# A spline evaluated from tables on TensorE: the far table is summed, and its part made, ahead of the near one

## The reference, cut to what matters

```python
out = relu(batchnorm(conv3x3(x, sign(w1)), gamma1, beta1))
out = batchnorm(conv3x3(out, sign(w2)), gamma2, beta2)
x = relu(out + x)                                  # the first layer's result

x_aff = clip(x * a[c] + b[c], -1.5, 1.5)           # the second layer, K = 32, R = 8
u = (x_aff + 1.0) * 0.5 * (K - 1)
i = floor(u); t = clip(u - i, 0, 1)
spline = sum over m of alpha_table[clip(i - 1 + m, 0, K - 1)] * b_m(t)      # four cubic basis functions
y = id_gain[c] * x + einsum('bchwr,cr->bchw', spline, mix) + bias[c]
```

## Time and profile before

| | |
|---|---|
| median of 3 runs | 1161.8 us (1159.59 to 1162.68) |
| time of the profiled execution | 1162.34 us |
| span of the profiled execution | 1160.5 us |
| TensorE matmuls busy | 1093.0 us |
| VectorE busy | 954.2 us |
| ScalarE busy | 909.4 us |
| chain that ended last | TensorE L1161 52%, L1170 8% |

### The profile page before, as it was taken

How to read it: one execution, slowest core, us unless ns; L and a number is a source line. 1 busy time by engine, 2 the same in 40 slices (tenths; PEclk the granted TensorE clock), 3 DMA queues, 4 the chain that set the end, 5 groups by cost and what they waited for, 6 DMA issues and landing times.

```text
span 1160.5 us, 51486 instructions
## 1 busy us (share of the span) xinstructions
PE 1093.0 (94%) x23818; PEld 751.4 (65%) x23818; DVE 954.2 (82%) x891; ACT 909.4 (78%) x451; POOL 138.6 (12%) x219
## 2 busy tenths in 40 slices
PE   6999999699999946999999999999999999999996
PEld 4678888578888833665666656665656766665664
DVE  5855656585665777999999999999999999999987
ACT  4435443678788627999999999999999999999971
POOL 7000000058000000011010110110110101101100
PEclk9999999899999977999999999999999999999998
DMA  6766765667767766899999989989999999999652
GB/s 229 260 257 256 278 241 224 229 236 279 278 256 281 289 249 169 189 218 228 220 218 230 218 214 236 220 216 237 215 220 222 213 230 212 225 217 219 147 134 85
DMA packets 58225, 260.95 MB, mean 225 GB/s; under 512 B 16336, under 2 KB 16336, under 8 KB 50000
## 3 DMA queue, kind: packets, MB, share of 16 engines
q1 hardware_dynamic: 48880, 209.20, 55.7%
q0 software_dynamic: 8640, 48.17, 22.7%
q10 hardware_dynamic: 544, 1.10, 0.3%
HBM read 104.29 MB, written 77.07 MB: 156 GB/s over the span
## 4 chain that ended last, share of the span: by engine, by line
PE 60%; DVE 1%; issue 1%; ACTq 0%; ACT 0%; DVEq 0%
PE tab L1161 52%; PE tab L1170 8%; ACTq L949 0%; DVE lin L1120 0%; DVE poly L1116 0%; DVE zbuf L1024 0%; DVE lin L1012 0%; DVE far_sq L1085 0%; DVE poly L1091 0%; DVE middle_mask L1046 0%; ACT zbuf L933 0%; ACT cell L941 0%; DVE lin L1018 0%; DVE offset L1032 0%; DVEq L1084 0%
## 5 line engine op out<-in xcount | busy, mean ns | idle before, releaser
L1161 PE MATMUL tab<-edge_mask,diag 128*32 128x392 bf16 x10240 | 446.8, 329 | 5.9 <-issue 5.9
L1161 PEld LDWEIGHTS tab<-edge_mask,diag 128*32 128x32 f16 x10240 | 277.1, 97 | 168.9 <-issue 28.4
L981 ACT ACTIVATE edge_mask<-cell,thr 128x6272 bf16<-128x6272 bf16 x62 | 338.6, 5508 | 0.5 <-DMA cell<-cell 0.5
L414 ACT ACTIVATE yout<-acc 128x1568 f32<-128x1568 f32 x64 | 94.2, 1472 | 163.0 <-PE acc L715 140.8
L1161 PE MATMUL tab<-middle_mask,diag 128*32 128x392 bf16 x4096 | 186.9, 332 | 26.8 <-DVE middle_mask L1046 22.9
L715 PE MATMUL acc<-band_split,w 64*64 64x392 f16 x4608 | 198.6, 330 | 9.9 <-ACT band_split L372 6.5
L715 PE MATMUL acc<-split,w 64*64 64x392 f16 x4608 | 196.5, 330 | 11.2 <-DVE w L467 9.7
L715 PEld LDWEIGHTS acc<-band_split,w 64*64 64x64 f16 x4608 | 164.3, 107 | 44.0 <-issue 14.8
L715 PEld LDWEIGHTS acc<-split,w 64*64 64x64 f16 x4608 | 154.5, 107 | 52.4 <-issue 11.8
L1161 PEld LDWEIGHTS tab<-middle_mask,diag 128*32 128x32 f16 x4096 | 110.3, 98 | 91.5 <-DVE middle_mask L1046 23.0
L524 DVE BATCH_NORM_STATS2 stats<-yout 128x392 f32 (+1 forms) x240 | 118.0, 555 | 60.8 <-ACT yout L414 60.0
(11 more groups left out here) (133 smaller groups left out, 956.2 us busy)
## 6 DMA issues: line engine op xcount, KB each, us to landing
y_scratch<-yout SPq DMA_DIRECT2D x32, 1568.0 KB, 6.2
cell<-cell SPq DMA_DIRECT2D x504, 98.0 KB, 5.0
xin<-y_scratch SPq DMA_DIRECT2D x16, 1568.0 KB, 9.1
lin<-far POOLq DMA_DIRECT2D x32, 784.0 KB, 9.5
out<-lin SPq DMA_DIRECT2D x31, 784.0 KB, 5.6
xin<-in_x SPq DMA_DIRECT2D x15, 1568.0 KB, 9.3
lin<-y_scratch SPq DMA_DIRECT2D x30, 784.0 KB, 9.5
lin<-in_x POOLq DMA_DIRECT2D x28, 784.0 KB, 7.7
```

Source lines behind the costliest of these rows:

```text
L414: act.activation(yout[b][:, :].rearrange("p (r k x) -> p k r x", r=2, k=TILES)[:, 2 * part:2 * part + 2], acc[:, 4 * part:4 * part + 4, 0: ...
L981: act.activation(mask_of(c, q)[:, :, :], cell4[c % 2][:, :, :], ACT.Sign, bias=thr[:, q:q + 1]).then_inc(sign_mask_ready, 1)
L1161: mm = pe.matmul(tab[(c + t) % 2][j * GROUP:(j + 1) * GROUP, sub, 0:SUB], keep["diag"][part][:, j % 2, t, q, :], mask_of(c, q)[:, j, sub * ...
```

## The change

The far table becomes the first table of a chunk and the near table the second. VectorE does `far_cube(c)` in the place where `near_cube(c)` stood, `far_part(c)` right behind `finish(c-1)`, and `near_cube(c)` behind `far_part(c)`. The first middle mask now waits for the near table, because that is the second one. By the new numbers `used(c, T_NEAR)` is 5c + 2 where it was 5c + 1, so the wait ahead of L1170 asks for the second table to have been used. The constants' small arrays are indexed by the same names, and the instructions that fill them stay as many.

```diff
-T_NEAR, T_FAR, T_SQ, T_LIN, T_VAL = range(TABLES)
+T_FAR, T_NEAR, T_SQ, T_LIN, T_VAL = range(TABLES)
...
             def middle(c, q):
 
                 dve.wait_ge(copied[c % 2], 256 * (c // 2 + 1))
-                dve.wait_ge(table_ready, used(c - 1, T_FAR))
+                dve.wait_ge(table_ready, used(c - 1, T_NEAR))
...
-                near_cube(c)
+                far_cube(c)
                 if c > 0:
                     finish(c - 1)
-                far_cube(c)
                 far_part(c)
+                near_cube(c)
                 if c + 1 < CHUNKS:
                     middle(c + 1, MIDDLE_QUADS[0])
                 square(c)
```

## The result

The changed kernel takes 1166.13 us (median of 20 executions, 1161.70 to 1168.02) against 1161.79 us for the kernel before on the same chips (20 executions, 1156.57 to 1169.46). The ratio is 1.0039, with a 95% interval of 1.0026 to 1.0051: slower by 0.4%, 4.3 us, where 9.5 us were forecast. The profiled execution took 1167.21 us, 4.87 us more than the one before.

The account below looks back on a forecast made before the run. TensorE's string of matmuls, 21.52 us a chunk, was taken as the bound; the change makes 29 x 22.12 + 6.12 = 647.60 us where there were 638.15, 9.45 more, so 1171.3 us, range 1164.5 to 1179.5.

Parts of the forecast that it names:

- The loop: Product at L1170, square, on to the next near_cube, product: 22.12 us a chunk, 0.60 us over TensorE's 21.52.
- chunks 30 and 31 don't pay: Without fixed and linear for a later chunk VectorE regains 2.0 us there; only chunks 1 to 29 pay.
- The handover: Near step to product's load 0.06 us, first load to next square 3.01 us; an exposed load adds at most 0.20.
- Nothing waits for far_sq, masks or the second table: At VectorE's steps and TensorE's mask loads, inputs come in time; the 0.54 us wait for the second table goes.
- The stops: TensorE's "issue" pieces, 14.07 us over 29 periods before; staying put, they exceed the new periods by 6.12 us.
- the sentence on `add_far`: GpSimd's far transfer is issued 2.5 us earlier in the chunk, while finish asks for it a whole chunk later.
- The second, in which the stops vanish behind the wait: Rival: TensorE's sequencer gets ahead while waiting, periods of 22.12 sharp, 3.3 us more, 1165.1 us; chance 0.10.
- Stops in full: Rival: no wait covers TensorE's stops, each of 29 periods gets 0.60 us, 17.4 us more, 1179.2 us; chance 0.13.
- faster: Rival: stops covered and a shorter loop through near_cube, 21.88 us a chunk, 3.6 us less, 1158.2 us; chance 0.04.
- it doesn't bite: Rival: TensorE reaches the product late enough in every chunk for other reasons, time unchanged at 1161.8 us; chance 0.06.

Follow-up runs that it names:

- e1: The changed kernel with near_cube put back ahead of far_part, the far table still first: 1161.77 us, ratio 0.9993 to the kernel before.
- e7: The changed kernel with GpSimd holding add_far until near_cube is done: 1170.31 us, ratio 1.0078 to the kernel before.
- e12: Repeat of e7 beside e11, the changed kernel with add_far held until near_cube is done: 1171.46 us, ratio 1.0075 to the kernel before.
- e11: The changed kernel once more, nothing altered, beside e12: 1165.73 us, ratio 1.0034 to the kernel before.
- e3: The changed kernel with add_far held until the next chunk's first middle mask is made: 1168.53 us, ratio 1.0059 to the kernel before.
- e2: The changed kernel with finish moved last, behind near_cube, and far_part_added split into one semaphore per buffer: 1150.75 us, ratio 0.9899 to the kernel before.
- e8: e2 with add_far held until near_cube is done: 1156.92 us, ratio 0.9961 to the kernel before.
- e6: e2 with add_far held until finish is done: 1161.09 us, ratio 1.0002 to the kernel before.
- e5: e1 with add_far held until the next chunk's first middle mask is made: 1170.15 us, ratio 1.0076 to the kernel before.
- e4: The kernel before with copies of the cells cut to 32 of 1568 pixels from chunk 2 on, for timing alone: 1149.72 us, ratio 0.9891.
- e10: The kernel before with its far transfer cut to 32 of 1568 pixels in every chunk, for timing alone: 1148.93 us, ratio 0.9893.

## Why the prediction was right in its mechanism and wrong in its size

**The loop: right.** 22.12 us were forecast for a period and 22.10 measured (19.03 from `square` to the end of the near step where 19.05 were forecast, then 0.06 and 3.01 as forecast); 0.5 us of wait at L1170, the 1.3 us of VectorE's wait ahead of `square`, and that chunks 30 and 31 don't pay, came as worked out. e1 shows that undoing the one move takes the loop away.

**The handover: right.** The product starts 0.06 us behind the near step, and from there to the next `square` it is 842.06 - 839.05 = 3.01 us, as in the earlier trace rows. No weight load came on top, with the wait or without it. The Trainium skill, in "TensorE: Matmul & The Clock Gate", section "Part 2: What happens when you issue a matmul", has the engine pull weight loads ahead of matmuls in flight; a wait that undoes this cost nothing here (0.20 us a chunk was the bound).

**Nothing waits for far_sq, masks or the second table: right.** VectorE has no such wait in the chunk shown. TensorE's weight loads wait for the middle masks 5.9 us in all from 465 to 1100 us, as they did before (5.7), and no matmul does.

**The stops: the step that failed.** I put 6.12 us of them over the new periods, "provided that the stops stay where they are"; 2.1 were measured, and 4.6 us less in 29 periods (643.03 against 647.60) is what the forecast was too high by, all but some tenths. (4.0 of the 4.6 are stops; the 0.02 us a period make 0.6.) They didn't stay, because of the sentence on `add_far`, which I had called harmless since `finish` asks for it only a chunk later. It is harmless to `finish`, but not to TensorE's stops.

The wait hides stops too, as forecast, and the trace says how many. Where TensorE loses nothing in a chunk it waits 0.51 us at L1170; where it does, it waits less or not at all:

```profile
921.46 5.78 PE L1161 MATMUL tab<-edge_mask,diag 128*32 128x392 bf16 x128
927.45 2.90 PE L1170 MATMUL tab<-poly,ident 128*128 128x392 f32 x8 [0.22 <-DVE poly L1056]
```

Those 128 matmuls take 5.49 us elsewhere; 0.29 us of a stop is hidden there. Summed over the 29 periods of the changed kernel (a period less 21.52, less the wait and the 0.07 us that an emptied TensorE adds to it), the stops are 5.65 us, of which the wait hides 3.52 and 2.13 show. Before they were 14.07. So the 4.88 us are made up of 16.82 for the loop (29 x 0.58), less 3.52 hidden, less 8.42 of stops that are gone; this divides the measured periods up and is no second measurement of them. The forecast had 7.95 hidden and none gone.

That the 8.42 went with the transfer's place, and not by the wait, e7 and e12 show: with the same order and wait and the transfer later, nearly all the stops are there again.

| far transfer issued | kernel with the wait | stops, us | of these hidden | median, us |
|---|---|---|---|---|
| 4.42 us ahead of the product's end | changed; e11 | 5.7; 5.0 | 3.5; 3.0 | 1166.13; 1165.73 |
| 2.41 ahead | e7; e12 | 12.9; 13.6 | 6.0; 5.8 | 1170.31; 1171.46 |
| 0.65 ahead | e3 | 7.9 | 5.6 | 1168.53 |

Without TensorE's wait, the earlier the transfer the fewer the stops:

| far transfer issued | kernel | stops, us | median, us |
|---|---|---|---|
| 5.47 us ahead of the product's end | e2 | 2.4 | 1150.75 |
| 2.97 ahead | e8 | 7.7 | 1156.92 |
| 1.46 ahead | e1 | 14.7 | 1161.77 |
| 1.33 ahead | before | 14.1 | 1161.79 |
| 1.21 ahead | e6 | 9.4 | 1161.09 |
| 0.55 behind | e5 | 30.8 | 1170.15 |

(The stops are of one execution each, the medians of 6 to 20; e6's profiled execution was its fastest, e1's and e5's their slowest.) The changed kernel's 5.7 and 5.0 us at 4.42 us ahead lie between e2's and e8's. Holding the transfer in the changed kernel brings the time to 1170.31 and 1171.46, beside the forecast of 1171.3. So the change was two: a loop that costs 16.8 us, less what it hides, and an earlier transfer that gives half of it back.

**The rivals.** The second, in which the stops vanish behind the wait (1165.1 us), came nearest in its number, but by luck: most of them were gone without the wait's doing, and e2 has no wait and as few. "Stops in full" is refuted by the stops that the wait hides, "faster" by the loop's 22.10, and "it doesn't bite" by the wait, which stands at L1170 in 25 of the 29 chunks.

**What a stop is.** The chain of the kernel before, at its longest "issue" and on, and the instruction queue's packets from 465 to 1100 us (packets, MB, share):

```profile
857.90 8.57 PE tab L1161 x203
866.46 1.45 issue
867.92 5.49 PE tab L1161 x128
873.41 0.18 issue
873.59 5.14 PE tab L1161 x117
```

```profile
q8 instruction: 103, 1.69, 1.2%
```

Between the two stops lie exactly 128 matmuls, with their weight loads 256 instructions. A packet of this queue is 16 KB, and 103 of them for some 29 chunks of 912 matmuls and loads make one for each 256. In the packets' times of that trace one landed at 866.48 and one at 872.23, 1.44 and 1.36 us ahead of the two restarts. It is so throughout: the 14 traces have 153 stops of 0.15 us and more between masks' matmuls from the first product to 1130 us, all a multiple of 256 instructions apart within one (counting 913 a chunk, one more than its matmuls and loads), and each ends 1.0 to 1.8 us behind the landing of a packet of this queue. Where such a count is passed without a stop, the last packet had landed 3.4 to 4.3 us before (the medians of the traces). So a stop is TensorE waiting for the next 256 instructions of its program. The packets ahead of the stops took no longer than the others (medians of 0.96 to 1.18 us against 0.96 to 1.26), but started later: 3.4 to 4.0 us behind the passing of the previous such count, against 0.5 to 2.1 (medians again).

**What stays open.** What such a packet waits behind before it starts, and so why the place of the far transfer matters, isn't shown; that it is other transfers on the same engines fits e4 and e10. Nor is the place a full rule: e3 has the transfer late and 7.9 us of stops, where e1 and e7 have 14.7 and 12.9.

## What to carry to other kernels

Where TensorE runs without a wait, add up the loop that a changed order closes, from start to start along the other engine's rows; here that gave the period within 0.02 us. But an earlier result also starts its transfer earlier, and with the transfer engines at 90% this was worth 8 us here and 11 in e2, to an engine that never waits for that transfer. When stops without a releaser stand in the chain, count the instructions between them, lay the instruction queue's packets beside them, and move or cut one large transfer at a time before counting them as fixed; the version found so (e2) is 1.0% faster than the kernel before, at the cost of one more semaphore.

## What the runs showed of the hardware that I had not expected

A transfer that TensorE doesn't wait for cost it some 12 us in 29 chunks: e10, with 16 KB instead of 784 KB in the far transfer, took 1148.93 us against 1161.79. The cost comes through TensorE's own program: it arrives in packets of 16 KB, 103 of them in 635 us, and each of the 153 stops in the 14 traces ends 1.0 to 1.8 us behind the landing of one.

GpSimd's issue of the same transfer took 1593 ns beside the bf16 middle mask and 860 ns beside float32 instructions of VectorE (the two L910 rows above), 1340 ns where it began 0.62 us into the mask instead of 0.38 (e7, at 843.75; before, at 835.05). In both it ended 0.12 to 0.13 us behind the mask's end. The Trainium skill, in "Trainium Architecture — The Big Picture", section "What this means for kernel authors", says that VectorE and GpSimd contend for one port pair, by an exclusive lock. The issue times agree with that; TensorE's stops did not follow them, as e8 and e10 show.
